# A transformer block's start: fill transposes, and statistics, values and `dd` in another order

## What is computed

```python
mod = (_silu(L0_c) @ L0_wmod).reshape(L0_c.shape[0], 6, 1, -1)
h = _layernorm(x, axis=-1) * (1 + ca) + sa
x = x + ga * _L0_attn_ref(h, ...)        # lax.scan over 8 blocks
h = _layernorm(x, axis=-1) * (1 + cb) + sb
x = x + gb * _L0_ffn_ref(h, ...)
```

```python
q, k, v = x @ Wq + bq, x @ Wk + bk, x @ Wv + bv
Q = elu(q) + 1;  K = elu(k) + 1
KV = sum_s(K * v);  Ksum = sum_s(K)
Z = 1.0 / (Q * Ksum + EPS_Z)
V = Q * KV * Z
x = _layernorm(gelu(V @ Wo + bo) + x, ln1_s, ln1_b)
h = gelu(x @ Wf1 + bf1)
x = _layernorm(gelu(h @ Wf2 + bf2) + x, ln2_s, ln2_b)
```

## Time and profile before

| | |
|---|---|
| median of 3 runs | 515.57 us (515.24 to 515.63) |
| the profiled execution's own time | 515.55 us |
| its span, first to last instruction | 513.7 us |
| TensorE busy | 498.7 us (97%) |
| VectorE busy | 428.3 us (83%) |
| ScalarE busy | 389.7 us (76%) |
| GpSimd busy | 260.9 us (51%) |
| granted TensorE clock | 1.00 |

### The profile page before, as it was taken

The page is one execution under the profiler, slowest core; times in us unless marked ns, Lnnn a source line. Parts: engine busy times, 40 slices in busy tenths (PEclk is TensorE's granted clock), DMA queues, the critical chain, the costliest instruction groups (busy, mean ns, idle before and its releaser), DMA issues.

```text
span 513.7 us, 8084 instructions
## 1 busy us (share of the span) xinstructions
PE 498.7 (97%) x1941; PEld 300.2 (58%) x1941; DVE 428.3 (83%) x1631; ACT 389.7 (76%) x586; POOL 260.9 (51%) x306
## 2 busy tenths in 40 slices
PE   8789999999999999999999999999998999999997
PEld 6345555555555555555555555555554666766676
DVE  5889888888898889888888988898888677886866
ACT  4768888888888888888888888888897953445453
POOL 3445655556665656666555556655553550213243
PEclk9999999999999999999999999999999999999999
DMA  8200010001000100010010001000100000707070
GB/s 246 98 17 1 7 42 15 0 5 41 15 5 2 39 15 5 21 24 12 5 41 15 0 5 41 15 5 9 32 1 1 1 1 0 165 20 175 12 183 23
DMA packets 19526, 17.51 MB, mean 34 GB/s; under 512 B 8604, under 2 KB 14236, under 8 KB 19508
## 3 DMA queue, kind: packets, MB, share of 16 engines
q1 hardware_dynamic: 18644, 16.58, 12.6%
q10 hardware_dynamic: 864, 0.73, 0.5%
HBM read 9.96 MB, written 1.05 MB: 21 GB/s over the span
## 4 chain that ended last, share of the span: by engine, by line
PE 87%; DVE 5%; ACT 2%; issue 2%; POOL 2%; DMA 1%; DVEq 0%; POOLq 0%
PE bank L457 19%; PE bank L448 14%; PE bank L323 12%; PE bank L470 5%; PE bank L611 5%; PE bank L445 5%; PE bank L365 4%; PE bank L370 4%; PE bank L366 4%; PE bank L568 3%; PE bank L570 3%; PE bank L569 3%; PE bank L685 1%; DVE hf L1172 1%; PE bank L692 1%
## 5 line engine op out<-in xcount | busy, mean ns | idle before, releaser
L457 PE MATMUL bank<-hid,wf 128*128 128x512 f32 x240 | 112.8, 592 | 0.0
L1032 POOL TENSOR_TENSOR rsD<-veD,c_half 128x4 f32<-128x4 f32 x32 | 37.8, 1180 | 119.6 <-DVE veD L1153 119.6
L448 PE MATMUL bank<-x,wf 128*128 128x512 f32 x180 | 87.2, 593 | 0.0
L846 ACT ACTIVATE hid<-bank,vbf 128x512 f32<-128x512 f32 x120 | 72.5, 694 | 0.0
L457 PEld LDWEIGHTS bank<-hid,wf 128*128 128x128 f32 x240 | 43.1, 190 | 43.2 <-issue 29.0
L448 PEld LDWEIGHTS bank<-x,wf 128*128 128x128 f32 x180 | 32.8, 189 | 31.8 <-DVE kk L1277 15.1
L1172 DVE TENSOR_SCALAR xhB<-bank,meanB,rsB 128x128 f32<-128x128 f32 x128 | 43.7, 405 | 8.6 <-POOL rsB L1032 8.6
L1243 DVE TENSOR_SCALAR x<-bank,vln 128x256 f32<-128x256 f32 x60 | 29.9, 539 | 22.4 <-PE bank L323 22.4
L1172 DVE TENSOR_SCALAR xhD<-bank,meanD,rsD 128x128 f32<-128x128 f32 x128 | 43.8, 405 | 5.4 <-POOL rsD L1032 1.1
L816 ACT ACTIVATE g<-bank,vbf 128x512 f32<-128x512 f32 x29 | 20.0, 688 | 34.8 <-PE bank L457 34.8
L323 PEld LDWEIGHTS bank<-ident,y 128*128 128x128 f32 x256 | 29.4, 140 | 27.2 <-POOL y L1052 12.4
(11 more groups left out here) (207 smaller groups left out, 1153.9 us busy)
## 6 DMA issues: line engine op xcount, KB each, us to landing
wf<-in_w_f SPq DMA_DIRECT2D x16, 256.0 KB, 2.6
hid<-kv_full SPq DMA_DIRECT2D x12, 256.0 KB, 4.3
x<-kv_full SPq DMA_DIRECT2D x9, 256.0 KB, 4.9
wu<-in_w_unit SPq DMA_DIRECT2D x10, 192.0 KB
wqkv<-in_w_qkv SPq DMA_DIRECT2D x7, 192.0 KB, 2.4
x<-in_x SPq DMA_DIRECT2D x4, 256.0 KB, 5.3
qk<-kv_full SPq DMA_DIRECT2D x3, 256.0 KB, 4.9
out<-ot SPq DMA_DIRECT2D x3, 256.0 KB, 2.6
```

Of the source, the lines that this page charges most:

```text
L448: mm = nc.tensor.matmul(ps_ff[j][:], wf1[:, j * P:(j + 1) * P], x2[(c - 2) % CH][:], start=True, stop=True)
L457: mm = nc.tensor.matmul(ps_f0[:], wf2[:, j, :], hid[:, j, :], start=(j == 0), stop=(j == FJ - 1))
L846: nc.scalar.activation(hid[:, j, :], ps_ff[j][:], ACT.Gelu_apprx_tanh, bias=vbf1[:, j:j + 1]).then_inc(h_ready, 1)
L1032: nc.gpsimd.tensor_tensor(rs[buf(k, n)][:], ve[buf(k, n)][:], c_half[:], ALU.pow).then_inc(rstd_ready[k], 1)
```

## The change

Only slots 0 to 2 and what stands ahead of them change; the loop and everything behind it have the same instructions in the same order.

- TensorE: 53 identity transposes instead of 16. Four become seven ahead of input 0's transposes; eleven are new behind them, eight ahead of Wo in slot 1, eight and seven in slot 2 behind input 3's transposes and behind those of `xhB`. The twelve of slot 1 stay, and follow input 2's transposes now.
- TensorE: the four products for the gates go from behind input 0's transposes to behind input 1's, at the end of slot 0. In slot 1 Wo comes ahead of input 2's transposes.
- ScalarE, slot 1 alone: `dd` ahead of `ek`.
- VectorE: the statistics of input 3 move from the front of slot 0 to behind its keys and values; `third_norm` moves from ahead of `vt` to behind it.

```diff
             modulate(ps_y, (0, 1))
-            keep_awake(4, ps_v)
+            keep_awake(7, ps_v)
             first_to_fm(0)
-            pe.wait_ge(ld["gates"], 16)
-            modulate(ps_d, (2, 3, 4, 5))
+            keep_awake(11, ps_v)
+
+            def second_input():
+                first_to_fm(1)
+                pe.wait_ge(ld["gates"], 16)
+                modulate(ps_d, (2, 3, 4, 5))
...
-            def second_fill():
+            def first_wait():
                 pe.wait_ge(mod_copied, 1)
+                keep_awake(8, ps_y)
+
+            def third_input():
+                first_to_fm(2)
                 keep_awake(12, ps_y)
 
-            slots(pe, slot, {"middle": lambda: first_to_fm(1)},
-                  {"behind the products": lambda: first_to_fm(2), "before ff2": second_fill},
-                  {"behind the products": lambda: first_to_fm(CH - 1)})
+            def fourth_input():
+                first_to_fm(CH - 1)
+                keep_awake(8, ps_y)
+
+            def second_wait():
+                keep_awake(7, ps_y)
+
+            slots(pe, slot, {"middle": second_input},
+                  {"behind the products": first_wait, "before ff2": third_input},
+                  {"behind the products": fourth_input, "start": second_wait})
...
+                second = isinstance(s, int) and s == 1
+                if has(a) and not second:
+                    keys()
                 if has(b):
+                    denominators()
+                if has(a) and second:
+                    keys()
...
                     vv.then_inc(v_ready, 1)
+                run(extra, "behind the values")
...
-            slots(dve, slot, {"before the last norm": lambda: first_stats(CH - 1)},
-                  {"before the last norm": third_norm, "behind the keys": gates_copied,
+            slots(dve, slot, {"behind the keys": lambda: first_stats(CH - 1)},
+                  {"behind the values": third_norm, "behind the keys": gates_copied,
                    "within the first norm": lambda: first_norm(CH - 1)},
```

More of the change, by code:

```diff
@@ L822, in slot, with keys @@
                     nc.scalar.activation(lden[:], qk[:], ACT.Ln, bias=c_eps[:, 0:1]).then_inc(lden_ready, 1)
-                if has(a):
+                def keys():
                     act.wait_ge(k_mm, a + 1)
@@ L827, in slot, with denominators @@
                     nc.scalar.activation(ek[:], ps_k[:], ACT.Exp, bias=va[:, 0:1]).then_inc(ek_ready, 1)
-                if has(b):
+                def denominators():
                     act.wait_ge(lden_ready, b + 1)
                     nc.scalar.activation(dd[:], lden[:], ACT.Exp, bias=c_lneps[:, 0:1], scale=-1.0).then_inc(dd_ready, 1)
+                second = isinstance(s, int) and s == 1
+                if has(a) and not second:
+                    keys()
+                if has(b):
+                    denominators()
+                if has(a) and second:
+                    keys()
                 if has(a):
```

## The result

The changed kernel takes 516.57 us (median of 21 executions, 516.39 to 516.75), the kernel before, timed beside it, 516.42 us (21 executions, 515.24 to 516.71). The ratio is 1.0013, with a 95% interval of 1.0007 to 1.0019: a slowdown of 0.1%, small and clear. It is not the ratio of the two medians, which differ by 0.15 us: the median of before lies at the lower edge of its upper group, and the means, 515.98 and 516.57, differ by 0.59.

A forecast was written before the change was run, and what follows sets the result against it. TensorE bounds behind 40 us, VectorE's queue the start: 22.56 + 0.47 (`third_norm` behind `vt`) + 0.88 (`mq` held) puts the statistics at about 23.85 instead of 23.26; 515.55 + 0.6 = 516.15 us, range 514.8 to 516.9.

The forecast's parts named there:

- What bounds, and which path binds: TensorE bounds behind 40 us; in the start VectorE's queue, later than `y1`'s transposes (22.68), sets `stB`'s statistics at about 23.85.
- The hold: VectorE's `mq`, reached at 20.91 while GpSimd runs `y1`, stands still until `y1` ends at 21.93: 0.88 us.
- The rule for its length: A held VectorE instruction waits for the running GpSimd instruction's end, less some 0.14 us of its own lead: 0.88 for `mq`.
- the second rival: `y1` starts 0.2 us or more later, `mq` comes first and `y1` waits: -0.03, 515.5 us; chance 0.12.
- The bound of 1.02: Upper bound in us for `mq`'s wait under `y1`, if no lead of its own is spared.
- `vt`'s start: On VectorE, about 0.1 us behind `dd`'s end: at 17.38 instead of 18.62, 1.24 us earlier.
- The fills' own cost: Identity transposes on TensorE, 0.11 us each, fit into its waits except three ahead of 7.75; taken as 0.
- They give nothing back either: The added identity transposes gain no time on TensorE, since no stretch shows the lower clock level: 0.
- the rival of the clock: Fills keep TensorE's clock up around 23 to 28 us, saving up to 1.4 us: 514.8 us; chance 0.09.
- The forecast of +0.6 us: `stB`'s statistics on VectorE start at about 23.85 instead of 23.26, moving the end equally: 516.15 us.
- The claim that the time stays within what can be told from no change: The whole kernel's change of 0.1% lies within the 0.2%, or 1.03 us, that a measurement tells; chance 0.78.

The follow-up runs named there:

- e4: The changed kernel with one wait more on GpSimd: in slot 1 `y1` starts only when `mq` is done; 515.99 us.
- e9: The changed kernel with four tiny VectorE memsets to the existing tile `sm` ahead of its first statistics; 515.92 us.
- e3: The changed kernel with `third_norm` put back ahead of `vt`, `dd` still ahead of `ek` and all fills kept; 515.37 us.
- the split version: The changed kernel with `third_norm` split: normalization of input 2 ahead of `vt`, variance of input 3 behind it; 514.72 us.

## Why the prediction was right or wrong

**What bounds, and which path binds: right.** Nothing changed behind 40 us but the moment of its start, and it was VectorE's queue, not `y1`'s transposes, that set the statistics of `stB`.

**The hold: right in mechanism, too small in size.** `mq` met `y1` and was held; the cost was 1.10 us, 0.88 in the sum. The rule for its length, `y1`'s end less `mq`'s start less 0.14, gives 22.39 - 21.15 - 0.14 = 1.10, to the hundredth. What was off is where they met. `y1` came 0.47 us later than worked out and `mq` 0.24, so that `y1` began 0.02 ahead of `mq` instead of 0.25. Most of this is `rsI`, which took 1.20 instead of 1.01 us: the lengthening named in the second rival, by nearly the 0.2 named there. That rival took it as enough to let `mq` go first; it was not, because `mq` came later as well, and it brought the hold to its longest instead. The bound of 1.02 was too low.

**`vt`'s start: wrong, 0.46 us.** The sum took 0.1 us from `dd`'s end to `vt`. It was 0.54 (the other 0.02 are `dd`'s), from a pause that the rows of before showed at `hf` (0.33, released by nothing) and that the prediction mentioned and left out of the sum. Four instructions more on VectorE remove it. The sum of the terms: 0.59 forecast for the statistics, + 0.46 for the pause, + 0.22 for the hold, - 0.11 for a closer sequence between `vt` and `stB` = 1.16, as measured. e4 takes away 0.58 us, e9 0.65, both together 1.23 of the 516.57, which brings it to the lower group. Not all of the 1.23 is the order's: from `nck` to the last wait of the start it is 23.21 us in the kernel before, 24.35 in the changed one and 23.31 with both parts taken away. So 1.04 of the 1.14 us are explained by experiment, and 0.27 of the 1.23 come from behind the loop.

**The fills' own cost: right.** No fill pushes what stands behind it, and their step is 0.11 us.

**"They give nothing back either": wrong.** This is the step that failed, and with it the argument against the rival of the clock. It read one execution, whose clock stayed up, and three times that lay within 0.4 us of each other. Of the kernel before, 11 of 21 executions beside the changed kernel and 26 of the 89 timed later lie in a group that is 1.1 us slower, and the one of them that was profiled has the lower level from about 28 to 32 us. With all the fills the group is gone. The rival's price, 1.4 us, was near, its place (two groups of transposes; it was the first feed-forward products) was not.

**The total.** The change is a cost of 1.1 us in each execution and a gain of 1.1 us in those that the upper group had; the ratio over all, 1.0013, is what is left. The forecast of +0.6 us, which is also the difference of the two means (0.59), came near it by luck: a cost taken 0.5 us too small, and a gain taken as nothing that came to 0.6 on the mean in this comparison, because 11 of the 21 lay in the upper group. The claim that the time stays within what can be told from no change didn't hold: 21 executions of each tell 0.1%.

What stays open: what the pause is (it goes with the place in VectorE's instruction stream, and the trace names nothing for it), and why an unused tile of 16 bytes a partition and four instructions shorten the part behind the loop, untouched by the change, by 0.67 and 0.21 us. The tile may move the addresses of later tiles, but no run shows that it is the address. What set `rsI`'s length was not isolated either. And neither the place of the clock's fall in the lower group's executions is shown, nor what lets it fall in some executions and not in others.

## What to carry to other kernels

Moving a value ahead on one engine moves its consumer on another: before taking it as a gain, lay the new times of GpSimd's long instructions beside VectorE's that read two operands in SBUF or go from SBUF to SBUF, since in these traces whoever came second stood still until the first was done; a wait that fixes the order can be faster than none. Look at the list of single times, not at one profile, before saying that fills buy nothing: two groups with a gap can be a clock that falls in some executions. The mean clock alone doesn't tell, as 22 of the 63 faster executions had it at 0.997 too; a profile of a slow one shows where it fell. Differences of 0.1% can come from an unused tile or a few instructions far from the edit, so an experiment at that scale needs its own control.

## What the runs showed that was not expected

- The clock can fall in a start where TensorE doesn't idle for long: in the profiled execution of the upper group TensorE was busy for 2.90 of the 4 us ahead of 28 us, with no wait above 0.92 us there, and the level was lower from 28 to 32 us. The execution of 515.55 us, with the same 2.90, kept the higher level. With 16 identity transposes only and the new order, waits of 1.31 and 0.93 us stood ahead of the fall, and it lasted for most of 8 us.
- Where the clock falls sets its price: 1.1 us at the first feed-forward products, 0.4 us at the products between 10 and 14 us, and 0.14 at most in the third of the lower group's executions with a lower mean clock, at a place that no profile shows.
- `rsI`, four elements a partition, took 1.20 us where it began 0.08 us behind `mk`'s start, 1.12 in e3, where it began 0.10 behind `vt`'s, and 1.01 in the kernel before, 0.03 behind `vt`'s.
- A pause of 0.33 to 0.44 us on VectorE, with no releaser, went away with four tiny instructions some 16 us ahead of it.
- An unused tile of 16 bytes a partition: -0.55 us on the changed kernel (516.57 to 516.02), -0.46 us on the split version (514.72 to 514.26).
